# Transposed one-hots by ScalarE instead of VectorE in a two-layer graph kernel, and the maxima of layer 1 taken one group earlier

## The reference

```python
# layer 0 (rows = src, cols = dst)
qE, kE, vE = (h[rows] @ Wq), (h[cols] @ Wk), (h[cols] @ Wv)    # 8 heads of 16
att = exp(clip(einsum('ehd,ehd->eh', qE, kE), -10, 10))
att = att / (segment_sum(att, rows)[rows] + 1e-8)
res = segment_sum(att[..., None] * vE, rows) + h
x = x + layernorm(res) * gamma + beta
# layer 1 (row = src, col = dst, and one more loop at each node)
alpha = beta * sum(h[row] * h[col], 1) / (norm[row] * norm[col])
alpha = exp(alpha - segment_max(alpha, row)[row])
out = segment_sum(alpha / segment_sum(alpha, row)[row] * h[col], row)
x = x + out
```

## Time and profile before

| | us |
|---|---|
| median of 3 runs | 5369.36 (5354.42 to 5392.84) |
| the profiled execution | 5351.34 |
| its span, first to last instruction | 5349.6 |
| DVE busy | 4343.4 (81%) |
| PE busy | 4241.9 (79%) |
| POOL busy | 3437.8 (64%) |
| ACT busy | 2006.9 (38%) |
| mean granted TensorE clock | 0.767 of full |

### The profile page before, as it was taken

How to read it: one execution, slowest core, us unless ns; L and a number is a source line. 1 busy time by engine, 2 the same in 40 slices (tenths; PEclk the granted TensorE clock), 3 DMA queues, 4 the chain that set the end, 5 groups by cost and what they waited for, 6 DMA issues and landing times. The chain is left out here.

```text
span 5349.6 us, 103650 instructions
## 1 busy us (share of the span) xinstructions
PE 4241.9 (79%) x23362; PEld 3510.8 (66%) x23363; DVE 4343.4 (81%) x12591; ACT 2006.9 (38%) x7682; POOL 3437.8 (64%) x3467
## 2 busy tenths in 40 slices
PE   5999957878787888777783588888888888888886
PEld 2788845656565666555562477777777777777776
DVE  7999968888888888888887677777877887778786
ACT  3999900000000000000004455555555555555554
POOL 0333367777777777777772576666766776666673
PEclk7999977676767666767765687887887887778786
DMA  1000033333333333333331322222222222222221
GB/s 46 17 25 22 16 90 101 101 101 102 102 101 101 101 101 102 101 101 102 101 101 38 60 52 48 50 49 47 50 50 48 50 51 48 48 47 50 47 52 49
DMA packets 172949, 357.55 MB, mean 67 GB/s; under 512 B 61770, under 2 KB 90830, under 8 KB 172690
## 3 DMA queue, kind: packets, MB, share of 16 engines
q0 software_dynamic: 136896, 330.76, 23.2%
q1 hardware_dynamic: 33958, 20.39, 1.4%
q10 hardware_dynamic: 1836, 4.03, 0.3%
HBM read 336.61 MB, written 15.12 MB: 66 GB/s over the span
## 5 line engine op out<-in xcount | busy, mean ns | idle before, releaser
L870 POOL DMA_INDIRECT h_rows<-h_table,idx_ring x1668 | 1589.5, 953 | 833.3 <-issue 479.0
L870 POOL DMA_INDIRECT kv_rows<-kv_table,idx_ring x1668 | 1652.6, 991 | 514.8 <-issue 507.7
L1047 PE MATMUL psum<-vx,hot 128*128 128x136 f32 x3336 | 865.4, 402 | 394.4 <-DVE acc L1078 375.6
L1047 PEld LDWEIGHTS psum<-vx,hot 128*128 128x128 f32 x3336 | 655.6, 270 | 589.8 <-DVE acc L1078 563.1
L1503 DVE SCALAR_TENSOR_TENSOR h_sb<-h_sb,corr,psum 128x129 f32 x1668 | 580.7, 348 | 441.5 <-PE psum L1460 169.0
L1003 ACT ACTIVATE vx<-clip 128x32 f32<-128x32 f32 x417 | 95.6, 229 | 2026.5 <-DVE clip L1118 2026.5
L1036 PE MATMUL psum<-q_sb,hotT 128*128 x3336 | 716.5, 382 | 50.1 <-DVE prod L1091 34.9
L1036 PEld LDWEIGHTS psum<-q_sb,hotT 128*128 128x128 f32 x3336 | 610.7, 274 | 193.9 <-issue 193.9
L1441 PE MATMUL psum<-q_sb,acc 128*128 x3336 | 572.7, 324 | 86.9 <-issue 86.9
L1441 PEld LDWEIGHTS psum<-q_sb,acc 128*128 128x128 f32 x3336 | 482.4, 223 | 202.1 <-issue 202.1
L1078 DVE TENSOR_TENSOR acc<-acc,psum 128x136 f32 x1668 | 485.2, 291 | 158.3 <-issue 33.4
(11 more groups left out here) (220 smaller groups left out, 5923.8 us busy)
## 6 DMA issues: line engine op xcount, KB each, us to landing
kv_rows<-kv_table,idx_ring POOLq DMA_INDIRECT x1668
h_rows<-h_table,idx_ring POOLq DMA_INDIRECT x1668
kv_table<-kv SPq DMA_DIRECT2D x21, 256.0 KB, 2.2
rows<-loc_rows SPq DMA_DIRECT2D x208, 4.0 KB
out<-q_sb SPq DMA_DIRECT2D x2, 1536.0 KB
h_sb<-h_now SPq DMA_DIRECT2D x21, 128.0 KB, 2.0
h_table<-acc SPq DMA_DIRECT2D x1, 1820.0 KB, 12.1
sorted_edges<-stage,addr POOLq DMA_INDIRECT x108, 2.9
```

The lines of the kernel that those rows point to most:

```text
L870: pool.indirect_dma_start(out=G[:, u, j, :], out_offset=None, in_=table, in_offset=bass.IndirectOffsetOnAxis(ap=idx[:, u, j:j + 1], axis=0 ...
L1047: last = nc.tensor.matmul(S_ps[j // HALF][:, j % HALF, :], hot[:, k, j * P:(j + 1) * P], vx[:, k, j, :], start=True, stop=True)
```

## The change

In both layers `hotT` is made by ACT instead of DVE. A new helper `own_row` does it in two instructions: Square of (`part_no` - number), written over the same PSUM bank, and then Relu of (1 - that), written to `hotT`; for whole numbers this gives 1.0 on a match and 0.0 elsewhere. The second waits on ACT's own semaphore for the first, so `s_hotT` counts two to a group, and PE's waits are doubled to match. In ACT's program the pair stands at the head of a step: ahead of the Exp in layer 0, and ahead of the logit in layer 1. POOL writes one column of ones (`one`) at the start of layer 0, and ACT waits for it once.

In layer 1 DVE takes the maxima three groups behind (`i - 3`) and not four, still ahead of the cosines. The scan of that group stays four behind.

```diff
+def own_row(act, nc, spread, part_no, one, out, s_hotT, count):
+
+    nc.scalar.activation(spread, spread, ACT.Square, bias=part_no[:, 0:1], scale=-1.0).then_inc(s_hotT, 1)
+    act.wait_ge(s_hotT, 2 * count - 1)
+    nc.scalar.activation(out, spread, ACT.Relu, bias=one[:, 0:1], scale=-1.0).then_inc(s_hotT, 1)
...
@@ layer 0, gpsimd
+            nc.gpsimd.memset(mem["one"][:, :], 1.0).then_inc(s_part, 1)
@@ layer 0, scalar
+            act.wait_ge(s_part, 2)
+
             def step(i, u, t):
+                if inside(i + 4):
+                    act.wait_ge(s_spread, i + 5)
+                    need(act, s_q, i + 5 - NEAR)
+                    own_row(act, nc, B_ps[u % 2], part_no, mem["one"], hotT[:, u % NEAR, :], s_hotT, i + 5)
                 if inside(i):
...
-            walk(act, step, RING0, first=0, drain=0)
+            walk(act, step, RING0, first=-4, drain=0)
@@ layer 0, tensor
-                    need(pe, s_hotT, i + 4)
+                    need(pe, s_hotT, 2 * (i + 4))
...
-                    pe.wait_ge(s_hotT, i + 4)
+                    pe.wait_ge(s_hotT, 2 * (i + 4))
@@ layer 0, vector
-            dve.wait_ge(s_part, 1)
...
-                if inside(i + 4):
-                    k = u % NEAR
-                    dve.wait_ge(s_spread, i + 5)
-                    need(dve, s_q, i + 5 - NEAR)
-                    nc.vector.tensor_scalar(hotT[:, k, :], B_ps[u % 2], part_no[:, 0:1], None,
-                                            ALU.is_equal).then_inc(s_hotT, 1)
...
-            walk(dve, step, RING0, first=-4, drain=4)
+            walk(dve, step, RING0, first=0, drain=4)
@@ layer 1, scalar
             def step(i, u, t):
+                if inside(i + 3):
+                    act.wait_ge(s_spread, i + 4)
+                    need(act, s_E, i + 4 - RING1)
+                    own_row(act, nc, B_ps[(u + 3) % 2], part_no, mem["one"], hotT[:, (u + 3) % RING1, :], s_hotT, i + 4)
                 if inside(i):
                     act.wait_ge(s_prod, i + 1)
...
-            walk(act, step, RING1, first=0, drain=7)
+            walk(act, step, RING1, first=-3, drain=7)
@@ layer 1, tensor: the two waits on s_hotT doubled in the same way
...
@@ layer 1, vector
-                if inside(i - 4):
-                    dve.wait_ge(s_L, i - 3)
-                    nc.vector.reduce_max(highs[:, ds(UPG * (i - 4), UPG), 1:2].rearrange("p u o -> p (u o)"),
-                                         L_ps[u % 2].rearrange("p (h e) -> p h e", h=UPG), AX_X).then_inc(s_gmax, 1)
+                if inside(i - 3):
+                    dve.wait_ge(s_L, i - 2)
+                    nc.vector.reduce_max(highs[:, ds(UPG * (i - 3), UPG), 1:2].rearrange("p u o -> p (u o)"),
+                                         L_ps[(u + 1) % 2].rearrange("p (h e) -> p h e", h=UPG), AX_X).then_inc(s_gmax, 1)
...
-                if inside(i + 3):
-                    dve.wait_ge(s_spread, i + 4)
-                    need(dve, s_E, i + 4 - RING1)
-                    nc.vector.tensor_scalar(hotT[:, (u + 3) % RING1, :], B_ps[(u + 3) % 2], part_no[:, 0:1], None,
-                                            ALU.is_equal).then_inc(s_hotT, 1)
-            walk(dve, step, RING1, first=-3, drain=9)
+            walk(dve, step, RING1, first=0, drain=9)
```

More of the change, by code:

```diff
@@ L1431, in step @@
                 if inside(i + 4):
-                    need(pe, s_hotT, i + 3)
+                    need(pe, s_hotT, 2 * (i + 3))
                     spread_row(pe, nc, RING1, (u + 4) % RING1, t + (u + 4) // RING1, B_ps[u % 2],
@@ L1437, in step @@
                     blks = [block_1_on(i, u, t, h) for h in range(UPG)]
-                    pe.wait_ge(s_hotT, i + 2)
+                    pe.wait_ge(s_hotT, 2 * (i + 2))
                     need(pe, s_prod, i)
@@ L1616, in program @@
             "part_no": sb("part_no", [P, 1]),
+            "one": sb("one", [P, 1]),
             "ident": sb("ident", [P, P]),
```

## The result

The changed kernel takes 5192.58 us (median of four runs, 5189.79 to 5194.99), the kernel before 5370.15 us beside it (5354.42 to 5392.84): a ratio of 0.9666, interval 0.9631 to 0.9701, so 178 us less. The profiled execution took 5194.99 us with a span of 5193.2 us; against the profiled 5351.34 us of before that is 156 us less.

The account below looks back on a forecast made before the run. Layer 0 was taken as bound by POOL, layer 1 by DVE at full clock, PE at half clock, and issue at loop turns. Savings of 0 + 82 + 65 = 147 us gave 5204, scaled to 5220 us; range 5150 to 5325 us.

Parts of the forecast that it names:

- such a scale: Whole kernel: the profiled execution lay 18 us under the runs' median of 5369 us, so 5204 us was raised to 5220 us.
- Part 1: Layer 0: the comparison leaves DVE, 311 us of work that turns into waiting for gathers; the pair hides in ACT's idle; 0 us.
- The bound of 64 us: Layer 0: gathers average 38 ns more than in layer 1, 0.15 us a group, so 64 us to gain or lose; taken as 0.
- Part 2: Layer 1, full clock: DVE's step shrinks by 0.66 us, from 4.63 to 3.97 us, and DVE no longer sets the pace.
- Part 3: Layer 1, full clock: ACT gains a pair of 1.52 us, its step becomes 4.30 us; groups fall from 4.63 us, saving 82 us.
- ACT nearly without a gap: Layer 1: expected sign of the forecast, full-clock groups of 4.3 us with ACT hardly idle.
- POOL binds in layer 1 too: Layer 1: rival, DVE waits for `h_rows` and 175 to 195 us are saved, 5175 to 5195 us; chance 0.26.
- bounded the gain at 195 us: Layer 1: the most it can gain before POOL binds, at 5.03 us a group.
- Part 4: Layer 1: earlier maxima save nothing directly but remove PE's 0.91 us wait; denser PE falls to half clock less, 65 us.
- not under 0.80: Layer 1: rival, PE's new short waits sink the clock below 0.80, gain 0 to 56 us, 5315 to 5369 us; chance 0.13.
- not 1.85: Layer 1, full clock: rival, ACT becomes the bound from a 1.85 us pair; at 1.99 us the kernel takes 5458 us; chance 0.08.
- no table load: Layer 1: rival, Square or Relu beside Exp costs two loads of 1283 ns a group, 560 us more, 5930 us; chance 0.01.

## Why the prediction held, and where it was wrong

The time, 5192.58 us, is in the range and 27 us under the forecast: the sum was 147 us, the profiled executions differ by 156, the medians by 178. (The profiled execution of before lay 19 us under its median, that of after 2 us over: such a scale can't be carried over.) But the sum came out well by luck, because two errors cancel: layer 0 was put 58 us too low, and the gain of layer 1 was put at 147 us and measured 202.

**Part 1 failed**: "DVE's work after a landing keeps its order and its distance from the gathers, so I take 0". The order stayed, but the wait for the landing moved off the product onto an instruction two places ahead, the distance grew by 0.15 us, and layer 0 lost 58 us. The bound of 64 us stood there, from the 38 ns by which gathers of layer 0 exceed those of layer 1; I hadn't asked which gathers those were. The single rows would have told: one in four at 1.11 us, always the one that starts in the multiply. That the pair on ACT is covered was right: ACT still waits 1474 us for the clip in layer 0.

**Part 2** held: where DVE sets the pace its step is about 4.0 us, as in the first rows of the last fence below (forecast 3.97).

**Part 3** held in kind. ACT in layer 1, after:

```profile
4002.27 0.63 ACT L906 ACTIVATE psum<-psum,part_no 128x512 f32<-128x512 f32 x1
4002.93 0.69 ACT L908 ACTIVATE acc<-psum,one 128x512 f32<-128x512 f32 x1
4004.34 0.30 ACT L1405 ACTIVATE logit<-cosb,cb_sb 128x4 f32<-128x4 f32 x1 [0.72 <-DVE prod L1519]
...
4009.39 0.30 ACT L1405 ACTIVATE logit<-cosb,cb_sb 128x4 f32<-128x4 f32 x1 [0.82 <-DVE prod L1519]
```

The pair takes 1.35 us, not 1.52: Square into its own PSUM bank 0.63 us (0.66 in layer 0) against my 0.69, and the wait between the two only 0.03 us, not the 0.14 taken from DVE's additions. But "ACT nearly without a gap" is wrong: it idles 0.72 and 0.82 us, and the group takes 5.05 us, not 4.30. DVE shows why (timeline of DVE, maxima and products):

```profile
4055.74 0.68 DVE L1540 TENSOR_REDUCE highs<-psum 128x512 f32 x1
...
4059.74 0.68 DVE L1540 TENSOR_REDUCE highs<-psum 128x512 f32 x1
...
4067.89 0.68 DVE L1540 TENSOR_REDUCE highs<-psum 128x512 f32 x1
...
4075.65 0.69 DVE L1540 TENSOR_REDUCE highs<-psum 128x512 f32 x1
4079.62 0.68 DVE L1540 TENSOR_REDUCE highs<-psum 128x512 f32 x1
...
4098.41 0.35 DVE L1519 SCALAR_TENSOR_TENSOR prod<-psum,h_rows 128x128 f32<-128x128 f32 x1 [1.04 <-DMA h_rows<-h_table,idx_ring]
...
4101.79 0.68 DVE L1540 TENSOR_REDUCE highs<-psum 128x512 f32 x1
4103.36 0.35 DVE L1519 SCALAR_TENSOR_TENSOR prod<-psum,h_rows 128x128 f32<-128x128 f32 x1 [0.89 <-DMA h_rows<-h_table,idx_ring]
...
4106.74 0.68 DVE L1540 TENSOR_REDUCE highs<-psum 128x512 f32 x1
```

The loop's turn costs a group of 7.76 us here (4067.89 to 4075.65), 8.8 us at the median of the 32 turns. Around it, the gathers have run ahead and groups take 4.0 us; once DVE has caught up, each takes 4106.74 - 4101.79 = 4.95 us, with a wait for the landing in each. That is POOL's floor: four gathers 1.25 us apart, 5.0 us a group. L1519 ran 1524 times in the window 3130 to 5030, so 381 groups, 4.99 us each (forecast floor 5.03). So **the rival "POOL binds in layer 1 too" took place**, at a chance of 0.26; its time of 5175 to 5195 us holds the result. Its layer 1 won 202 us, and layer 0 gave 58 back. I had bounded the gain at 195 us; the gathers were 6 ns shorter than the 953 ns I used, 10 us over the layer.

**Part 4 was under-sized.** The 65 us for the clock became 74 to 91 us for the shift of the maxima alone; the clock had risen from 0.81 to 0.84 with the one-hots already. The half-clock share of the window fell from 0.38 of 2100 us (798 us) to 0.26 of 1900 (494 us; clock 0.87), as forecast in sign. Whether the shift works through the clock or through PE's wait itself isn't separated: both changed together, and POOL's floor cuts the sum off.

The other rivals: the clock of layer 1 was 0.84, not under 0.80; the pair took 1.35 us, not 1.85; there is no table load between Relu and Exp in either layer, both kernels have five in all. The Trainium skill (ScalarE: Activation LUTs, Rules for kernel authors) would have left relu and mul with VectorE. At 1.35 us the pair is dearer than the 0.745 us comparison, and yet layer 1 gains by it, 128 us without the shift, since DVE was the bound.

## What to carry to other kernels

When an instruction is taken out ahead of a wait, ask which instruction will carry that wait now, how long after the event the work behind it will start, and what other traffic it will meet. Here 0.15 us of late start, in a loop where each group meets the gathers at the same point, cost 58 us, with the engine 18% lighter. Look at the single instances of a group whose mean exceeds its median, and name what runs beside the long ones, before calling a cost zero. When two layers show their engines within 10% of each other, compute the floor of each next engine, take the cap as the likeliest outcome if several edits push towards it, and size the edits against it rather than one by one.

## What the runs showed of the hardware

- A gather that starts while DVE runs a 128x512 instruction with both operands in SBUF ends 0.82 us after that instruction does, where this is later than its usual end (medians of 0.817 to 0.823 us in the traces of all four sets, for the f32 multiply, the f32 comparison and the bf16 comparison), and otherwise takes 0.944 to 0.949 us. Products read from PSUM, reductions, and ACT's work show no such effect.
- From a landing to the instruction that waits for it DVE took 0.024 us where that instruction carries the wait itself, 0.123 us where the semaphore instruction ahead of it does, and 0.181 to 0.196 us where a register instruction two ahead does, each time with DVE idle. The source does not decide this alone: the same three lines gave the first in the kernel before and the last in the changed one.
- Square of 128x512 f32 within one PSUM bank took 0.63 us in layer 1 and 0.66 us in layer 0, Relu from PSUM to SBUF 0.687 us; the second started 0.03 us after the first ended, though it waits for it by semaphore.
- The kernel before took 5370 and 5374 us in two sets and 6792 and 6913 us on the chips of two others. On the last two it had long stalls, and relieving DVE in layer 0 gained there what it cost elsewhere.
